# Attention: the young group's products turned by the Vector engine in 32x32 squares, and the plan's K passed through DRAM in float32

## What is computed

```python
qn = q / (norm(q) + 1e-8)
log_K = -(1 - qn @ qn.T) / 0.1            # diagonal: -1000 / 0.1
for _ in range(10):                       # Sinkhorn
    log_u = log_marg - logsumexp(log_K + log_v[None, :], axis=-1)
    log_v = log_marg - logsumexp(log_K + log_u[:, None], axis=-2)
z = exp(log_u[:, None] + log_K + log_v[None, :])
z = z / max(z); z[diagonal] = 1
out = softmax(z * scale) @ v
```

## Time and profile before

| | us |
|---|---|
| median of 3 runs | 4948.91 (4929.03 to 4949.96) |
| the profiled execution, its own time | 4951.83 |
| its span | 4949.8 |
| busy: PE, PEld | 4509.5, 3619.3 |
| busy: DVE, ACT, POOL | 3790.9, 3104.7, 309.8 |
| L699, products (58368 matmuls), busy | 1694.2 |
| L709, turns, PE busy | 513.6 |
| L830, copies of y on ACT, busy | 347.4 |
| L977, K joined again on DVE, busy | 467.7 |

### The profile page before, as it was taken

The page is one execution under the profiler, slowest core; times in us unless marked ns, Lnnn a source line. Parts: engine busy times, 40 slices in busy tenths (PEclk is TensorE's granted clock), DMA queues, the critical chain, the costliest instruction groups (busy, mean ns, idle before and its releaser), DMA issues. The chain is left out here.

```text
span 4949.8 us, 191559 instructions
## 1 busy us (share of the span) xinstructions
PE 4509.5 (91%) x84325; PEld 3619.3 (73%) x84326; DVE 3790.9 (77%) x8677; ACT 3104.7 (63%) x4620; POOL 309.8 (6%) x347
## 2 busy tenths in 40 slices
PE   5999999975899999999999999999999879599992
PEld 3777777742588888888888888888888745277771
DVE  8999999944488888888888888888888746355556
ACT  4777777732566666666666666666666325377776
POOL 0000000000000000000000000000000005433331
PEclk9999999997899999999999999999999979699996
DMA  1001000023001111111121112100000024322224
GB/s 65 29 31 38 28 28 28 17 94 82 25 16 34 29 34 33 30 28 23 38 46 37 39 42 53 27 23 17 17 18 13 7 90 161 129 67 69 69 68 163
DMA packets 190199, 232.93 MB, mean 47 GB/s; under 512 B 81024, under 2 KB 159104, under 8 KB 187328
## 3 DMA queue, kind: packets, MB, share of 16 engines
q1 hardware_dynamic: 175872, 189.76, 14.2%
q0 software_dynamic: 13632, 32.66, 1.8%
HBM read 144.09 MB, written 78.25 MB: 45 GB/s over the span
## 5 line engine op out<-in xcount | busy, mean ns | idle before, releaser
L699 PE MATMUL y_ps<-k_sb,x_sb 128*12 128x256 f16 x58368 | 1694.2, 273 | 44.1 <-DVE x_sb L958 29.7
L699 PEld LDWEIGHTS y_ps<-k_sb,x_sb 128*12 128x12 bf16 x58368 | 1457.4, 88 | 184.0 <-DVE x_sb L958 38.2
L830 ACT ACTIVATE y_sb<-y_ps 128x256 f32<-128x256 f32 x912 | 347.4, 381 | 675.7 <-PE y_ps L699 675.7
L839 ACT ACTIVATE k_new<-cos,k_bias 128x512 f32<-128x512 f32 x768 | 520.3, 682 | 172.5 <-PE cos L726 172.5
L709 PEld LDWEIGHTS turned_x<-rows_in,y_sb 128*128 128x128 f32 x3648 | 471.3, 191 | 101.9 <-issue 51.8
L988 DVE CUSTOM_DVE_ANT_0 plan<-plan,u_rows,v_last 128x512 f32<-128x512 f32 x768 | 535.9, 745 | 8.2 <-issue 0.6
L257 PE MATMUL acc<-w_hl,feat_h 128*128 128x384 f16 x2688 | 455.4, 327 | 87.5 <-ACT feat_h L242 87.5
L709 PE MATMUL turned_x<-rows_in,y_sb 128*128 128x16 f32 x3648 | 513.6, 258 | 8.4 <-ACT y_sb L830 8.3
L1003 DVE TENSOR_TENSOR k_sb<-k_new,k_sb 128x2048 f16<-128x2048 f32 x192 | 439.3, 2288 | 66.5 <-ACT k_sb L847 62.4
L853 ACT ACTIVATE plan<-plan,p_bias,p_scale 128x1024 f32<-128x1024 f32 x384 | 464.5, 1238 | 12.2 <-DVE p_scale L999 12.2
L977 DVE TENSOR_TENSOR plan<-k_sb 128x1024 f32<-128x1024 f16 x384 | 467.7, 1218 | 0.0
(11 more groups left out here) (259 smaller groups left out, 7122.1 us busy)
## 6 DMA issues: line engine op xcount, KB each, us to landing
x_in_sb<-expert_rows SPq DMA_DIRECT2D x39, 528.0 KB
xt<-in_x_dram SPq DMA_DIRECT2D x16, 1280.0 KB, 6.0
q_left<-q_parts SPq DMA_DIRECT2D x192, 64.0 KB, 3.9
q_right<-q_parts SPq DMA_DIRECT2D x192, 64.0 KB, 4.0
raw<-in_w_dram SPq DMA_DIRECT2D x24, 384.0 KB, 4.4
w<-w_halves SPq DMA_DIRECT2D x16, 576.0 KB, 7.4
w<-expert_results SPq DMA_DIRECT2D x24, 384.0 KB, 5.9
v_parts<-v_sb SPq DMA_DIRECT2D x16, 408.0 KB, 2.4
```

The costliest lines, as they stand in the source:

```text
L699: last = nc.tensor.matmul(y[a][32 * c:32 * c + XW, :, :], high[:, j, XW * h:XW * (h + 1)], k_sb[s][:, h, :, at:at + P], start=(h == 0 and ...
L830: nc.scalar.activation(y_sb[a][:, :, :], y[a][:, :, :], ACT.Copy).then_inc(rows_read[a], 1)
L839: nc.scalar.activation(k_new[h % 2][:, c, :], cos[:, c % 2, :], ACT.Exp, bias=k_bias[:, 0:1], scale=1.0 / (REG * Q_SCALE ** 2), accum_out= ...
```

## The change

- **Young product.** The strips take other columns of K. Strip c now gets, of each block b of 128 tokens, the 32 tokens 32c to 32c+31: the moving operand is a pattern of 8 runs of 32 float16 (2 halves, 4 blocks) in place of 2 runs of 128. With that, turning each 32x32 square of `y_ps` in place puts the token on the right partition.
- **Young turn.** `next_x` on DVE waits for the product itself: a `transpose` of 128x256 from PSUM into `turned_y`, a `tensor_reduce` over the three parts and two halves (96 values to 16), then `split` as before. ACT's `read_rows(0)` and PE's `turn(0)` are gone; the old group keeps both. In DVE's order, `next_x` now stands ahead of `scale_of`.
- **K for the plan.** SP stores each chunk of `k_new` to a ring of five groups in DRAM (`store_k`, 256 KB each, 16 in a phase) and loads it again two or three phases later into `plan` (`load_k`, 16 in a phase); `plan` has four buffers instead of two. `join` is gone. `times_u` waits for the load, ACT's first exponential of a head waits until the stores of the head two before have landed, and ACT's `high_parts` no longer waits for `join`.
- **SP's order.** Its loads and stores of K are spread over the rounds, each round held until the young x of the round before is there.
- **End of a phase.** The `split` of the first row sums moves ahead of the last `low_parts`; the first young product of a phase now waits for `k_built` too.
- SP clears the counters of the stage before at its start.

```diff
@@ attend
-        plan = two("plan", [P, TB, TOKENS], F32)
+        plan = [sb(f"plan{h}", [P, TB, TOKENS], F32) for h in range(GH)]
+        turned_y, y_sum = sb("turned_y", [P, 2 * P], F32), sb("y_sum", [P, TB, GH], F32)
+        parts_of_y = turned_y[:, :].rearrange("p (two b r) -> p b r two", two=2, b=TB)[:, :, 0:XW, :].rearrange(
+            "p b (h k) two -> p b h two k", h=GH)
@@ SP
+            def store_k(G, h, chunks):
+                H = (G + 1) * GH + h
+                for c in chunks:
+                    after(sp, k_exp, H * TB + c + 1)
+                    sp.dma_start(k_all[(G + 1) % RING, h, c, :, :], k_new[h % 2][:, c, :]).then_inc(k_out[h % 2], 16)
+
+            def load_k(F, h, chunks):
+                if chunks[0] == 0:
+                    after(sp, pv_ready, (F - 1) * GH + h + 1)
+                    after(sp, k_out[h % 2], 16 * TB * ((F * GH + h) // 2 + 1))
+                for c in chunks:
+                    sp.dma_start(plan[h][:, c, :], k_all[F % RING, h, c, :, :]).then_inc(k_in[h], 16)
@@ SP, phase
+                for i in range(CYCLES):
...
+                    if young and i > 0:
+                        after(sp, x_new[0], G * YOUNG + i - 1)
+                    if i in LOADS_OLD and fin:
+                        load_k(G - 2, *LOADS_OLD[i])
+                    if i in LOADS_NEW and old:
+                        load_k(G - 1, *LOADS_NEW[i])
...
+                    if build:
+                        store_k(G, *((a, (0, 1)), (a, (2, 3)), (b, (0, 1)), (b, (2,)), (b, (3,)))[c])
@@ PE, multiply
+                    after(pe, k_built, (G + 1) * GH)
...
-                            at = j * TOKENS + c * P
+                            to, at = y[a][32 * c:32 * c + XW, :, :], j * TOKENS + c * P
+                            moving = k_sb[s][:, h, :, at:at + P]
+                            if a == 0:
+                                to = to.rearrange("p two (b i) -> p two b i", b=TB)
+                                moving = k_sb[s][:, h, :, :].rearrange("p two (j b c i) -> p two j c b i", j=TB, b=TB, c=TB)[:, :, j, c]
@@ PE, phase
-                    if young and i > 0:
-                        turn(0, G * YOUNG + (i - 1))
@@ ACT
+                        after(act, k_out[h % 2], 16 * TB * (H // 2))
-                    if young and i > 0:
-                        read_rows(0, G * YOUNG + (i - 1))
@@ DVE
+            def next_x(n, s):
+                after(dve, product[0], n + 1)
+                nc.vector.transpose(turned_y[:, :], y_ps[0][:, 0:2 * P]).then_inc(y_turned, 1)
+                after(dve, y_turned, n + 1)
+                nc.vector.tensor_reduce(y_sum[:, :, :], parts_of_y, AX_XY, ALU.add).then_inc(y_summed, 1)
+                after(dve, y_summed, n + 1)
+                split(y_sum[:, :, :], s, x_steps[0], n, x_new[0])
-                            join(G - 2, new, a, 0)
...
+                    if i == CYCLES - 1 and build:
+                        after(dve, k_exp, (G + 2) * (GH * TB))
+                        split(row_sums[new][:, :, :], new, first_steps, G + 1, first_x)
                     if c == 4 and build:
                         low_parts(G, new, b)
...
-                if build:
-                    split(row_sums[new][:, :, :], new, first_steps, G + 1, first_x)
```

More of the change, by code:

```diff
@@ L667, in phase @@
                     load_v(t - 1 if s == 0 else t, (s + 2) % 3)
-                if tail:
-                    after(sp, att_ready, (G - 2) * GH)
-                    store(t - 1, s)
+                for i in range(CYCLES):
+                    f, c = i // 5, i % 5
+                    a, b = 2 * f, 2 * f + 1
+                    if young and i > 0:
[4 more added lines that the diff above has]
+                        load_k(G - 1, *LOADS_NEW[i])
+                    if i == 4 and tail:
+                        after(sp, att_ready, (G - 2) * GH)
+                        store(t - 1, s)
+                    if build:
+                        store_k(G, *((a, (0, 1)), (a, (2, 3)), (b, (0, 1)), (b, (2,)), (b, (3,)))[c])
+            for counter in over:
+                sp.sem_clear(counter)
             sp.wait_ge(zeroed, START + ZEROS)
@@ L697, in multiply, with turn @@
                         for c in range(TB):
[L698 to L700 removed]
+                            to, at = y[a][32 * c:32 * c + XW, :, :], j * TOKENS + c * P
[3 more added lines that the diff above has]
+                                moving = k_sb[s][:, h, :, :].rearrange("p two (j b c i) -> p two j c b i", j=TB, b=TB, c=TB)[:, :, j, c]
+                            last = nc.tensor.matmul(to, high[:, j, XW * h:XW * (h + 1)], moving,
                                                     start=(h == 0 and j == 0), stop=(h == GH - 1 and j == TB - 1))
                 last.then_inc(product[a], 1)
[L704 to L707 removed]
+            def turn(n):
+                after(pe, rows_read, n + 1)
+                after(pe, x_new[1], n)
                 for part in range(2):
[L709 to L710 removed]
+                    last = nc.tensor.matmul(tr_flat, y_sb[:, part, :], add_parts, start=(part == 0), stop=(part == 1))
+                last.then_inc(turned, 1)
             def turn_x(G, s, build):
@@ L826, in _, with read_rows @@
             act.wait_ge(consts, START + CONSTS)
-            def read_rows(a, n):
-                after(act, product[a], n + 1)
-                nc.scalar.activation(y_sb[a][:, :, :], y[a][:, :, :], ACT.Copy).then_inc(rows_read[a], 1)
+            def read_rows(n):
+                after(act, product[1], n + 1)
+                nc.scalar.activation(y_sb[:, :, :], y[1][:, :, :], ACT.Copy).then_inc(rows_read, 1)
             def exponents(G, s, h, chunks):
@@ L851, in weights @@
                     after(act, scale_ready, F * GH + h + 1)
-                part = plan[h % 2][:, 2 * half:2 * half + 2, :]
+                part = plan[h][:, 2 * half:2 * half + 2, :]
                 nc.scalar.activation(part, part, ACT.Exp, bias=p_bias[:, 0:1], scale=p_scale[h % 2][:, 0:1]).then_inc(p_ready, 1)
@@ L912, in phase @@
                         if build:
[L913 removed]
+                            high_parts(G, new, b)
             phases(act, phase)
@@ L1051, in phase @@
                     a, b = 2 * f, 2 * f + 1
+                    if young and i > 0:
+                        next_x(G * YOUNG + (i - 1), mine)
                     if c == 2 and fin:
@@ L1055, in phase @@
                         scale_of(G - 2, b)
-                    if young and i > 0:
-                        next_x(0, G * YOUNG + (i - 1), mine)
                     if c == 0 and f == 1 and G == MAX_PHASE:
```

67 lines of the change are left out of this document (28 added, 39 removed).

## The result

The changed kernel takes 4893.19 us (median of 5 runs, 4886.07 to 4903.58), the kernel before, run beside it on the same chip, 4948.91. The ratio is 0.9893, with a 95% interval of 0.9878 to 0.9908: faster by 1.1%, 56 us, where 153 us were forecast. The time lies just above the range of 4735 to 4890.

The account below looks back on a forecast made before the run. PE was taken to bound the attention, DVE not far behind. Turn -173, copy +10, wait on x +14, boundary -8 and first phase +1 sum to -156 us off the profiled 4951.8: 4796 us, range 4735 to 4890.

Parts of the forecast that it names:

- K through DRAM: K's 16 stores and 16 loads of 256 KB a phase: counted as nothing, hidden by SP's idle time.
- Rival 4: Gain mostly lost to uncounted waits, on ACT's copy or PE's own issue beside fuller DMA engines: 4890 us; chance 0.05.
- its two conditions: Conditions given for the range's lower end, 4735 us: turns at 0.47 us each and no waits on x.
- Turn, 173 us: Young turns taken off PE: 432 at 0.40 us each, -173 us (-156 to -203), all on the path.
- Copy of the old product: PE waits on ACT's copy, formerly covered by the young turn: 0.17 us in round 4, 0.05 in round 5; +10 us.
- Chain on DVE: Transpose, reduction and split take 1.46 us; PE waits 0.5 us for x before round 6 in 28 phases, +14 us.
- Boundary: Wait before a phase's first young product: 0.64 becomes 0.2 us in 28 phases, none becomes 0.2 in 19; -8 us.
- E: The end of a pair of products on PE, from which the forecast counted times; at the boundary, that of round 9.
- DVE as the bound: Rival: transpose or reduction takes twice its price, so PE waits for x, +30 to +60 us, 4826 to 4856; chance 0.13.
- The scattered moving operand: Rival: runs of 32 float16 slow the 432 young products; 5185 us at 50% more, 5574 at half rate; chance 0.07.
- SP's queue: Rival: 32 K issues at 1.92 us each make SP's queue the bound, 67 us a phase, +570, 5520 us; chance 0.04.
- The estimate of 2.6 us for one K transfer: Rule against the forecast: 32 K transfers one after another take 83 us, more than a phase; by the rows, zero.

## Why the prediction was wrong

**The step that failed** is "K through DRAM", priced at zero: "I count nothing; SP's idle time hides it." I asked of the transfers whether they are in time and whether SP and the DMA engines can carry them, and they can: no row product waits for K, and the share is 0.60 to 0.63, below the 0.67 worked out. I did not price what else goes over the DMA engines: PE's instructions, whose packets now start a median of 1.41 us into the block before and not 0.42. The term that I put at nothing measures 111 us. Rival 4 named it, "PE's own issue beside fuller DMA engines", at a chance of 0.05 and 4890 us. The time came out at 4893, but that closeness is luck: the 2 us a phase of the rival were an example, worked out from nothing. The trace of before had the sign of it: 14 us of issue idle, of which 13 lie just behind the q loads, at a DMA share of only 0.14 over the stretch. The mean share says little; 64 KB loads, eight in a row, already starved PE.

**The rest of the sum held.** Without the transfers the phase is 51.93 us, forecast 51.9, and the time 4782 against 4796. (Taken off the median and not off the profiled execution, the sum gives 4793. The lower end of the range, 4735, does not follow from its two conditions, which give 4742 to 4752.) Term by term, in the changed kernel's timelines, PE:

```profile
2067.59 0.49 PE L778 MATMUL u_rows<-eye_four,head_max 128*128 128x128 f32 x2
2068.15 0.62 PE L748 MATMUL turned_x<-rows_in,y_sb 128*128 128x16 f32 x4
...
2073.74 0.40 PE L772 MATMUL u_rows<-xt_sb,pick 128*128 128x128 bf16 x4
...
2074.29 0.62 PE L748 MATMUL turned_x<-rows_in,y_sb 128*128 128x16 f32 x4
2074.93 3.67 PE L739 MATMUL y_ps<-k_sb,x_sb 128*12 128x256 f16 x128
...
2094.98 0.33 PE L756 MATMUL cos<-eye_bf,x_sb 128*120 128x128 bf16 x2
...
2100.48 3.67 PE L739 MATMUL y_ps<-k_sb,x_sb 128*12 128x256 f16 x128
```

and one chain on DVE:

```profile
2088.43 0.44 DVE L996 STREAM_TRANSPOSE turned_y<-y_ps 128x256 f32<-128x256 f32 x1
2088.90 0.25 DVE L998 TENSOR_REDUCE y_sum<-turned_y 128x16 f32<-128x96 f32 x1
2089.19 0.26 DVE L988 RECIPROCAL x_sb<-y_sum 128x16 f32<-128x16 f32 x1
...
2089.70 0.19 DVE L992 TENSOR_TENSOR x_sb<-x_sb 128x16 f32<-128x16 f32 x1
```

- *Turn, 173 us.* Not measured by itself. The phase without transfers is 3.24 us shorter, and with the waits below (0.35, and 0.14 in the phases with weight pieces) and some 0.3 gained at the boundary the turns come out near 0.37 us each, an estimate; 0.40 was taken.
- *Copy of the old product.* In round 4 the turn starts 0.56 us after the maximum's row instead of 0.32, so it waits 0.24 (forecast 0.17); in round 5 it starts 0.55 after the small turn's row instead of 0.44, so 0.11 (0.05). That makes 16 us instead of 10.
- *Chain on DVE.* Transpose 0.444, reduction 0.253, whole chain 2088.43 to 2089.89, 1.46 us: all as taken. The estimate of 0.44 us from the Trainium skill, "VectorE: DVE Perf Modes", section "The three transpose paths", agrees with the 0.444. The wait before round 6 is 2074.29 to 2074.93 less 0.50, some 0.14 us, where I had 0.5: DVE was less late than I counted.
- *Boundary.* Round 1's products start 5.50 after E (2094.98), forecast 5.39 + 0.2 = 5.59.

**The rivals.** DVE as the bound is no matter in the change; it is in the run with the join on DVE. The scattered moving operand costs nothing: 274 ns against 273. The rule of the Trainium skill, "Advanced Engine Details and Errata", section "SBUF Cachelines", by which accesses within a line of 16 bytes go at the full rate, agrees with this for runs of 64 bytes. SP's queue is not the bound, but its stalls matter in another way: what piles up behind a wait leaves as a burst. The estimate of 2.6 us for one K transfer and 83 us for 32 in a row, from the Trainium skill, "DMA: Bandwidth & Descriptors", section "Anatomy of one DMA", did not come true as a price: a transfer lands 3.1 or 3.6 us after its issue, and 32 of them fit into 54 us, since they overlap. That section is about DMAs that GpSimd issues; these are SP's.

## What to carry to other kernels

A transfer that is hidden from the engine that uses it can still hold up the engine that doesn't: look in the waits for idle time put down to "issue", see where in the loop and where in the engine's list it lies, and hold that against the DMA queue's timeline. Spread DMAs over the rounds of a loop, and put no wait for a late buffer in front of others that could go: here that alone gave back 94 us at the same bytes. Before moving work to an idle engine, see what it does to the length of the other engine's operations.

## What the runs showed of the hardware

- Copies from DRAM to DRAM, at a DMA share of 0.4, stop PE in the middle of a product for up to 3.1 us (64 us in 65 gaps), and loads to SBUF do the same (57 us in 67). Stores of the same size hardly do (25 us in 28 gaps, against 14 us in 18 without any K transfer).
- PE's instructions come in packets of 16 KB, one for 256 instructions. In this case's twelve traces every issue gap of the attention (508) lies at the start of such a block and ends a median of 1.4 us behind the end of its packet. Beside K's transfers the median packet is not longer (1.06 us, 1.08 before) but starts later (1.41 us into the block before, against 0.42).
- The same traffic costs 46 us in one kernel (a phase of 55.17 us without it) and 111 in the other (51.93). The fetches start less late in the first (1.01 us against 1.41); why stays open.
- GpSimd's float16 joins, 2.66 us each, lengthen some of DVE's two-input operations by more than their own length in the mean (190 to 440 ns, 1012 to 2890 ns) and leave others alone (the row products stay at 744 ns, the low parts at 2285). A small subtraction beside a join takes 1.30 us in the mean, any other 0.19. Why some are spared no run here shows.
